# Counting most of the repeated edge class beside the edge stage's chunks instead of in the bucket stage

## The reference, cut to what matters

```python
src = jnp.concatenate([edge_index[0], loops]); dst = jnp.concatenate([edge_index[1], loops])
e = leaky_relu(a_src[src] + a_dst[dst], 0.2)
ee = exp(e - segment_max(e, dst)[dst])
denom = segment_sum(ee, dst)
agg = segment_sum(h[src] * (ee / denom[dst])[:, :, None], dst)   # -> norm, top 2 of 4 gates
out = sum_e gate_e * (gelu(x @ W1[e] + b1[e]) @ W2[e] + b2[e])
```

## Time and profile before

| | |
|---|---|
| median of 3 runs | 3792.41 us |
| the profiled execution's own time | 3804.78 us |
| its span on the core | 3803.2 us |
| PE busy | 2755.2 us (72%) |
| DVE busy | 2363.9 us (62%) |
| ACT busy | 1368.9 us (36%) |
| POOL busy | 1076.1 us (28%) |
| bucket block's count of the class | 599 to 735 us |
| edges block's chunks | 1878 to 2467 us |

### The profile page before, as it was taken

How to read it: one execution, slowest core, us unless ns; L and a number is a source line. 1 busy time by engine, 2 the same in 40 slices (tenths; PEclk the granted TensorE clock), 3 DMA queues, 4 the chain that set the end, 5 groups by cost and what they waited for, 6 DMA issues and landing times. The chain is left out here.

```text
span 3803.2 us, 55281 instructions
## 1 busy us (share of the span) xinstructions
PE 2755.2 (72%) x16302; PEld 1674.2 (44%) x16302; DVE 2363.9 (62%) x4497; ACT 1368.9 (36%) x2278; POOL 1076.1 (28%) x1034
## 2 busy tenths in 40 slices
PE   0432126879999999995577775025999999949994
PEld 0432125734444444442444554014566565526662
DVE  9999898677777888877633333387434444443333
ACT  5310100067777877875434443024001000002221
POOL 0000100177777400000155565400011111214442
PEclk9999999989999999998588888555999999979997
DMA  5999891055454545443111111162333333324446
GB/s 199 357 377 410 309 411 63 9 195 183 166 187 163 214 158 192 177 183 98 23 42 46 43 44 40 6 210 89 101 106 105 106 107 108 107 65 130 125 127 190
DMA packets 233149, 567.75 MB, mean 149 GB/s; under 512 B 52065, under 2 KB 93384, under 8 KB 224446
## 3 DMA queue, kind: packets, MB, share of 16 engines
q1 hardware_dynamic: 145318, 375.39, 28.8%
q10 hardware_dynamic: 56152, 163.80, 11.6%
q0 software_dynamic: 31552, 27.13, 3.2%
HBM read 442.65 MB, written 125.39 MB: 149 GB/s over the span
## 5 line engine op out<-in xcount | busy, mean ns | idle before, releaser
L1781 PE MATMUL at_out<-at_pt,top_H 128*128 128x512 f32 x2048 | 935.2, 603 | 43.6 <-DVE at_pt L1709 29.6
L1623 ACT ACTIVATE at_rl<-at_qrow,at_less,at_steep 128x512 f32<-128x512 f32 x1024 | 742.4, 804 | 104.6 <-DVE at_pt L1709 66.1
L1709 DVE SCALAR_TENSOR_TENSOR at_pt<-at_rl,at_turned 128x1024 f32<-128x1024 f32 x512 | 626.3, 1223 | 163.6 <-PE at_out L1781 81.3
L1998 PE MATMUL at_out<-at_parts,at_a 128*128 128x387 bf16 x4096 | 688.8, 329 | 21.8 <-DVE at_parts L2071 15.7
L1781 PEld LDWEIGHTS at_out<-at_pt,top_H 128*128 128x128 f32 x2048 | 374.2, 191 | 450.3 <-issue 394.8
L1998 PEld LDWEIGHTS at_out<-at_parts,at_a 128*128 128x128 fp8e4 x4096 | 399.6, 98 | 297.9 <-issue 28.3
L896 POOL DMA_INDIRECT rec<-at_part x304 | 377.5, 1242 | 107.0 <-issue 95.3
L1138 POOL DMA_INDIRECT edges_GT<-tab,gat_RC x320 | 327.5, 1023 | 253.1 <-DMA edges_GT<-tab,gat_RC 158.6
L1946 POOL DMA_INDIRECT slots<-at_Y,at_dest x128 | 123.2, 963 | 645.1 <-DVEq L2176 609.1
L645 PE MATMUL pack_bp<-top_weights,sort_recs 128*128 128x8 bf16 x1696 | 75.8, 169 | 234.0 <-DMA sort_recs<-in_adj_dram 234.0
L2449 PE MATMUL ex_hp<-ex_XS,ex_WB 128*128 128x512 f32 (+1 forms) x472 | 217.4, 597 | 1.9 <-DMA ex_WB<-wts 1.9
(11 more groups left out here) (543 smaller groups left out, 3585.2 us busy)
## 6 DMA issues: line engine op xcount, KB each, us to landing
sort_recs<-in_adj_dram SPq DMA_DIRECT2D x212, 512.0 KB, 8.9
at_adj<-in_adj_dram SPq DMA_DIRECT2D x192, 512.0 KB
adjT<-at_turned ACTq DMA_DIRECT2D x64, 1024.0 KB
at_a<-adjT SPq DMA_DIRECT2D x128, 512.0 KB
bucket_raw<-in_adj_dram ACTq DMA_DIRECT2D x120, 512.0 KB, 10.2
ex_WB<-wts SPq DMA_DIRECT2D x42, 533.0 KB
y<-f_YB ACTq DMA_DIRECT2D x64, 256.0 KB
f_YB<-y SPq DMA_DIRECT2D x16, 1024.0 KB, 10.8
```

Of the source, the lines that this page charges most:

```text
L1623: ins = nc.scalar.activation(RL[v % NBUF][:, k, :], qrow[:], ACT.Relu, bias=less[:], scale=steep[:, u:u + 1])
L1709: nc.vector.scalar_tensor_tensor(out=PT[v % NBUF][:], in0=RL[v % NBUF][:], scalar=1.0, in1=AT[v // VP % 2][:, 2 * (v % VP):2 * (v % VP) + ...
L1781: ins = nc.tensor.matmul(OUT[:], H[:, u, :], PT[v % NBUF][:, k, :], start=(u == 0), stop=(u == T - 1))
L1998: ins = nc.tensor.matmul(OUT[:, g, x, 0:3 * D1], ones[c % NBUF][:, j, x * P:(x + 1) * P], parts[:, u].rearrange("p k d -> p (k d)"), start ...
```

## The change

Of the 2048 columns of each half, the bucket block now counts only those behind the first `HELD` = 464 (58 groups of 8); its trip count becomes the old one less 58, at least 1. The first 464 columns of both halves are stored to DRAM (`classes`) by SyncE in the bucket block and loaded again in the edges block. There they are counted in 29 sets. A set is 4 pairs of one-hots on VectorE (`count_hots`) and 32 products on TensorE (`count`) that form a sum of their own in the last 64 columns of the look-up's PSUM bank (`HIST`); VectorE adds each finished sum to a table `total` (`add_counts`), which starts as `repeat`. 17 sets belong to the 16 leading chunks (one made ahead of the loop, one counted between the loops), 12 to the 4 late chunks, three for each. PE's look up now also waits for `same_read`, that is, until VectorE has added the chunk before's sum. The steps with `twin`, `den` and half of `A` move behind the chunks. VectorE's loop of 5 rounds becomes two loops (0 to 4, 4 to `rounds`). The hots lie in the buffers YB[4] to YB[7], which nothing uses in this block.

```diff
+GC = 8
+EARLY_SETS, LATE_SETS = 17, 12
+HELD = (EARLY_SETS + LATE_SETS) * 2 * GC
@@ pack, DVE
                     groups_of(3, scr[0:1, 5:6], GC)
+                    step(nc.vector.tensor_scalar(ctl[0:1, 3:4], ctl[0:1, 3:4], float(HELD // GC), 1.0, ALU.subtract, ALU.max))
@@ bucket, SP
                     sp.dma_start(H[:], stored_rows).then_inc(rows_in, 16)
+                    for k in range(2):
+                        sp.dma_start(classes[:, k], both[:, k, :].rearrange("p (b c) -> p b c", b=2)[:, :, 0:HELD]).then_inc(classes_out, 16)
@@ bucket, DVE
-                            cols = bass.ds(i * GC + b * HC, GC)
+                            cols = bass.ds(i * GC + b * HC + HELD, GC)
@@ edges, SP and POOL
+                    sp.dma_start(kept, classes).then_inc(classes_in, 16)
                     sp.wait_ge(tab_out, 16)
...
+                    nc.gpsimd.iota(value, pattern=[[1, P], [0, GC]], base=0, channel_multiplier=0,
+                                   allow_small_or_imprecise_dtypes=True).then_inc(value_ok, 1)
                     pool.wait_ge(tab_out, 16)
@@ edges, DVE
+                    def count_hots(s, at, done):
+                        for n in range(PAIRS):
+                            cols = bass.ds(at * (2 * GC) + n // 2 * GC, GC)
+                            ins = one_hots_across(nc, OFC[s][n], OPC[s][n], value, kept[:, 1, n % 2, cols], kept[:, 0, n % 2, cols], T, GC)[1]
+                        ins.then_inc(done, 1)
+
+                    def add_counts(used, number):
+                        dve.wait_ge(used, number)
+                        dve.sem_inc(passed, 1)
+                        now(nc.vector.tensor_tensor(total[:], total[:], HIST, ALU.add))
+                        dve.sem_inc(same_read, 1)
+
+                    def late_hots(g, r):
+                        for i in range(g * IN_LATE, (g + 1) * IN_LATE):
+                            dve.wait_ge(late_used, (off + r) * LATE_SETS + i + 1)
+                            dve.sem_inc(passed, 1)
+                            count_hots((1 + i) % 2, EARLY_SETS + i, late_hot)
...
+                        if not leading:
+                            late_hots(g, r)
                         dve.wait_ge(gt_in[g], (off + r) * (16 * CK) + 16 * CK)
...
                         gather_sums(g, k + 1)
+                        if leading:
+                            add_counts(same_used, l * EARLY_SETS + r * RG + g + 1)
+                            count_hots((g + 1) % 2, r * RG + g + 1, same_hot)
+                        else:
+                            add_counts(late_used, (off + r) * LATE_SETS + (g + 1) * IN_LATE + 2)
...
+                            if lo == 0:
+                                add_counts(same_used, l * EARLY_SETS + EARLY_SETS)
...
+                        now(nc.vector.tensor_tensor(twin, twin, total[:].unsqueeze(2).to_broadcast([P, T, NH]), ALU.mult))
                         now(nc.vector.tensor_tensor(den[:], own, twin, ALU.add))
-                        now(nc.vector.tensor_tensor(heads(A[:, 0]), heads(rows[:, :, 0:HE]), over(own), ALU.mult))
                         now(nc.vector.tensor_tensor(heads(A[:, 1]), over(twin), heads(among(lastrow[:, 0:HE], T)), ALU.mult))
                         now(nc.vector.tensor_tensor(A[:, 0], A[:, 0], A[:, 1], ALU.add))
@@ edges, PE
+                    def count(s, some, opens, closes):
+                        for n in some:
+                            for c in range(GC):
+                                ins = nc.tensor.matmul(HIST, OPC[s][n][:, :, c], OFC[s][n][:, :, c], start=(opens and n == 0 and c == 0),
+                                                       stop=(closes and n == PAIRS - 1 and c == GC - 1), skip_group_check=True)
+                        return ins
...
+                                pe.wait_ge(same_read, k + l + 1)
                                 look_up(k, g)
                                 for e in range(1, NE):
                                     hidden(u + e, e)
+                                    if e == 2:
+                                        early_ready(l * EARLY_SETS + q, k)
+                                        count(g % 2, range(PAIRS // 2), True, False)
                                     output(u + e - 1, e - 1)
+                                    if e == 2:
+                                        count(g % 2, range(PAIRS // 2, PAIRS), False, True).then_inc(same_used, 1)
                                     if e == 3:
                                         scatter(k, g)
                                 output(u + NE - 1, NE - 1)
+                        early_ready(l * EARLY_SETS + EARLY_SETS - 1, (off + LEAD) * RG - 1)
+                        count((EARLY_SETS - 1) % 2, range(PAIRS), True, True).then_inc(same_used, 1)
                         with pe.Fori(LEAD, rounds) as r:
                             for g in range(RG):
+                                pe.wait_ge(same_read, k + l + 2)
                                 look_up(k, g)
+                                late_counts(g, r, k)
                                 scatter(k, g)
```

145 lines of the change are left out of this document (95 added, 50 removed).

## The result

The changed kernel takes 3701.19 us (median of 4 runs, 3695.55 to 3702.64) where the kernel before, on the same chip, takes 3793.72: a ratio of 0.9758, 95% interval 0.974 to 0.9775. Measured again on another chip it takes 3677.35 against 3768.58 us: 0.9747 (0.9726 to 0.9767). So it is faster by 91 to 95 us. The forecast was 0.9716, or 108 us; the range and the sign hold, and 13 to 17 us of the gain are missing.

The account below looks back on a forecast made before the run. The prediction took the class count to stand alone in the bucket stage and POOL's gathers to bound the edge stage's leading chunks. Terms: -133.0 + 0.2 + 20.9 + 3.6 = -108 us, so 3685 us (chance 0.60), range 3661 to 3726.

Parts of the forecast that it names:

- The bucket term: Bucket stage: the class count stands alone on the path; 55 iterations of 2.418 us go, -133.0 us.
- rival 5: Bucket stage: the trip count would not fall, so the change does not do what it says; chance 0.01.
- rival 1: Edge stage swallows the counts, no gather delayed, clock rises: edge stage +8, sum -125, 3668 us; chance 0.14.
- rival 3: Edge stage: POOL locked out for whole sets, gathers 110 us longer, sum about -19, 3773 us; chance 0.02.
- rival 4: Edge stage: hots, products and addition serial for each set, 244 us, sum +111, 3903 us, slower than before; chance 0.03.
- The leading chunks: Edge stage, first 16 chunks: sets fit the gaps; hots delay gathers 0.5 us a set, 8.5 us over 17 sets.
- the slack: Leading chunks: each may grow 2.7 us on other engines before it is later than its gather; a set adds 1.3.
- rival 2: Leading chunks: TensorE becomes the bound, a chunk grows 2 to 3 us, sum -68 to -75, 3720 us; chance 0.20.
- the rows of L1156: Edge stage: a gather under VectorE's one-hots took 2.15 us, ending 0.83 us after them; read as descriptor writing clashing.
- Between the loops: Between leading and late chunks: set 17's hots, products and addition are serial ahead of the look-up, 8.2 us on the path.
- Late chunks: Last four chunks: sums to logits 13.1 us, on to the next sums 16.2, pace 29.3 against 29.7; -1.2 in three.
- Moved steps: Behind the last chunk: four steps cost 3.3 us and the last addition 0.3, nothing covers them, +3.6 us.

Follow-up runs that it names:

- the three later versions that have the same leading chunks: Changed kernel without the set between loops (3666.02 us); that plus some late hots moved a chunk earlier (3668.86); without that set, last steps in the last wait (3657.74).
- the fastest version: Changed kernel without the set between the loops, late sums and the four table steps put in the wait for the scatter: 3657.74 us, ratio 0.9707.
- products twice: Each leading set's 32 products done twice, against a version without the set between loops and with some late hots moved a chunk earlier: 3747.44 us, ratio 0.9938.

## Why the prediction was right, and where it was short

**The bucket term held.** 55 x 2.418 less the small steps gave -132.8; the stage lost 130.7 and 136.1 us, and its start varies by 2 to 3 us between executions of the same kernel. The trip count fell to one iteration, so rival 5 is out.

**Rivals 1, 3 and 4** did not come as times: the edge stage lost 34 us and not 8; the gathers' busy time rose by 12.4 and 8.0 us and not 110; and of 29 sets only the one between the loops is wholly serial. But two of their conditions did: the clock in the leading chunks rose (0.84 to 0.88), as in rival 1, and single gathers were held for a whole set of hots, as in rival 3 (5.20 us). The prediction's reading that a gather waits only for the VectorE operation in progress does not hold for these.

**The leading chunks: near the forecast in one profile of two, and not for its reason alone.** The forecast put 8.5 us there for delayed gathers; the pairs of profiles gave +20.6 and +9.1. Gathers are delayed, by 0.2 to 0.5 us a set. But whether the stream gets longer by it differs: from the first to the last gather it took 575.9 us before and 574.0 after in the first pair, 569.6 and 581.4 in the second, and 582.1 in the kernel before with the split loop, which has no hots. In the first profile of after the gathers can't be the reason. What the leading part lost there is a lag of the other engines' chain behind the gathers, and it differs from execution to execution: 441 to 449 us in the two profiles before, 446 and 455 in two versions without sets, 450 and 469 in the two after, and 442 to 452 in the three later versions that have the same leading chunks.

The step that was read wrongly is the slack. The prediction took it as 2.7 us from VectorE's waits for gathers. The same reading gives 2.6 us when all four late waits are taken as they are (6.4, 13.9, 14.8 and 13.4), 3.8 in the kernel before's second profile, and more with the sets than without: VectorE waits for gathers 40.9 us in the 16 leading chunks before and 64.8 in the fastest version. Such a wait tells how far a chunk is ahead, not what it can take each time. By the pace with half of the gathers the slack was 4.5 us (24.3 against 28.8), of which up to 1.7 came with the higher clock. The prediction also took a set for 1.3 us of a chunk; there it is 3.3, as only one gap was left to use and as the new wait for the addition costs 1.1. The two errors nearly cancel, by luck: 27.6 us forecast as 27.4. But 1.2 us below the gathers' pace means, by estimate, that a chunk which is late by 10 us stays late for eight chunks. This fits the loss in the first profile, where VectorE stopped waiting for gathers after chunk 7; what made single chunks late there (35.0, 34.9 and 37.5 us) was not tested. It is also the reason why rival 2, with 0.20, was nearer than its number: products twice put the chain past the bound at once.

By the Trainium skill (SBUF — State Buffer, section "Who interferes with whom") a VectorE instruction with two SBUF inputs contends with a GpSimd instruction that reads SBUF, while descriptor generation is inferred not to clash with it. The lengthened gathers above (1033 to 1168 ns on average, one of 5.20 us) agree with the first. They don't settle the second: a gather also reads its indices (gat_RC) from SBUF, and no run separates the two. So where the prediction says that the rows of L1156 speak against the inference, it says too much.

**Between the loops** the mechanism was right and the size 8.2 instead of 10.0 us: 3.8 of hots and 4.1 of products were as costed, but the two additions took 0.8 and 1.1 us with their hand-overs, where 0.3 each stood, and 0.4 came ahead of the products. In the second profile the last scatter was late too, so that the stretch took 40.5.

**Late chunks.** L1239 to L1248 was to be 13.1 us; it was 15.2 and then 14.0, 13.6 and 13.5, since the third set's hots waited until 2253.47 for the first one's products. From L1248 to the next L1239 the prediction took 16.2 us, but its own terms give 15.07 + 2.9 - 1.2 = 16.8, and the -1.2 stood on TensorE at full clock, which was wrong (0.50). Measured are 15.3 us, so that the pace of 29.0 us (29.9 in the second profile) was as forecast (29.3) with some luck: the look-up's second half, which came late before (rows of before in the earlier trace rows: L1225 at 7.1 us behind the transposes), now comes 3.7 us behind them.

**Moved steps:** +4.0 and not +3.6: the four steps take 3.4 us (3.3 forecast), and the addition adds 0.6 with its hand-overs, where 0.3 had been put down.

**What was missing** is attend_route's +5.6 and, in the sum, the hand-overs. Without attend_leaky the profiles' mean change is -92 us, 16 short of the forecast: 6.3 are the leading chunks, 5.6 attend_route, 2.3 the place between the loops, 1.2 the first late chunk, 1.0 combine_project and 0.4 the moved steps; the rest is below 1 us a term. How much of the 6.3 belongs to the kernel and how much to the one late execution, two profiles can't divide.

## What to carry to other kernels

Work that moves beside a loop costs its own time minus the gaps that it really meets, plus every new wait; read the slack from the pace that the other engines would have alone, not from the waits for the slowest one, and measure it by halving that one's work. Look at the granted clock in both runs, since it differs between them. What is left at the seams of loops is serial and costs its full length: give the last iteration's product to the next loop instead of counting it between. And a loop written twice on one engine can cost a few us in a stage that it doesn't touch, here 5.

## What was not expected of the hardware

A gap between TensorE's recorded end and the start of VectorE's instruction that reads the result, of 3 to 4 us where 0.15 is usual and without any other wait in the profile, appears in both kernels (up to 3.1 us before, 4.2 after). In the version with one product of 32, a late chunk's look-up and its reader are

```profile
2246.48 0.36 PE L1438 MATMUL edges_lk<-gat_near,edges_OHT 128*128 128x12 bf16 x8 [0.56 <-ACT edges_OHT L1350]
2250.78 0.36 DVE L1239 TENSOR_REDUCE edges_adv<-edges_lk 128x64 f32<-128x192 f32 x1 [8.10 <-DMA at_qs<-srow]
```

and in the changed kernel, at the same granted clock of 0.50,

```profile
2272.02 0.36 PE L1438 MATMUL edges_lk<-gat_near,edges_OHT 128*128 128x12 bf16 x8 [0.55 <-ACT edges_OHT L1350]
2272.53 0.36 DVE L1239 TENSOR_REDUCE edges_adv<-edges_lk 128x64 f32<-128x192 f32 x1 [4.31 <-PE edges_lk L1438]
```

3.94 us from end to start in the one, 0.15 in the other. With 31 products less a set the late chunks were longer by the logits, 30.8 us against 29.0 and 29.9. In the first profile of after the gaps of 3.19, 3.73 and 2.60 us ahead of the sums of chunks 7, 11 and 14 lie in chunks of 35.0, 34.9 and 33.2 us, so they have a part in its lag or are a sign of it. The ends of matmuls are modelled, so the record can be early; what holds the signal back, and why it does so with less work on TensorE, stays open.
